# Selective-scan mixer: y and the gate computed transposed, norm weights folded into the output weights, score rings of three banks

## What is computed

```python
gate, hBC, dt = split(x_n @ in_proj_w.T)          # 8192, 10240, 128 wide
hBC = silu(causal_conv(hBC, conv_w, 4 taps) + conv_b)
hs, Bm, Cm = hBC                                  # 128 heads of 64; 8 groups of 128
dt = clip(softplus(dt + dt_bias), 0, 100); A = -exp(A_log)
# per chunk of 128 tokens, cum = cumsum(dt * A):
Y_diag = (C B^T * exp(cum_l - cum_s), l >= s) @ (hs * dt)
Y_off  = exp(cum) * (C @ state)
Y = Y_diag + Y_off + hs * D
g = Y * silu(gate)                                # per group of 1024 columns:
out = g * rsqrt(mean(g*g) + eps) * norm_w
y = out @ out_proj_w.T
# attention, 32 heads of 16: softmax(q k^T / 4, causal) @ v
```

## Time and profile before

| | |
|---|---|
| median of 3 runs | 3235.74 us (3235.0 to 3238.88) |
| the profiled execution's own time | 3237.73 us, span 3235.9 us |
| TensorE, VectorE, ScalarE, GpSimd busy | 91%, 63%, 32%, 20% |
| TensorE clock granted, mean | 0.966 |
| mixer, 64 slots | 141 to 2320 us |
| experts, first pass | 2365 to 2480 us |
| attention, heads | 2667 to 3040 us |
| experts, second pass | 3110 to 3236 us |

### The profile page before, as it was taken

The page is one execution under the profiler, slowest core; times in us unless marked ns, Lnnn a source line. Parts: engine busy times, 40 slices in busy tenths (PEclk is TensorE's granted clock), DMA queues, the critical chain, the costliest instruction groups (busy, mean ns, idle before and its releaser), DMA issues. The chain is left out here.

```text
span 3235.9 us, 41691 instructions
## 1 busy us (share of the span) xinstructions
PE 2954.3 (91%) x12832; PEld 1668.3 (52%) x12832; DVE 2040.1 (63%) x3246; ACT 1035.7 (32%) x2401; POOL 654.9 (20%) x438
## 2 busy tenths in 40 slices
PE   3799999999999999999999999999879978888889
PEld 2455555555555555555555555555468443333478
DVE  5666666666666676666666676675364647777464
ACT  1233233233233233233333232232221325666421
POOL 1222132222212222221221222222121000000021
PEclk7899999999999999999999999999989888999989
DMA  4001010010001001001010100100010420111000
GB/s 164 15 2 37 1 56 24 14 56 14 23 13 45 24 13 56 15 23 55 2 35 4 56 25 13 55 1 2 10 60 0 164 75 30 37 37 34 6 7 20
DMA packets 55890, 106.97 MB, mean 33 GB/s; under 512 B 24385, under 2 KB 27537, under 8 KB 53009
## 3 DMA queue, kind: packets, MB, share of 16 engines
q1 hardware_dynamic: 50384, 102.60, 9.4%
q10 hardware_dynamic: 5312, 2.00, 0.3%
HBM read 85.71 MB, written 18.87 MB: 32 GB/s over the span
## 5 line engine op out<-in xcount | busy, mean ns | idle before, releaser
L443 PE MATMUL bank<-xnT,wh 128*128 128x512 f32 x1280 | 571.7, 598 | 60.7 <-DVE sg L832 30.0
L587 PE MATMUL bank<-wo,ggT 128*128 128x512 f32 x1024 | 469.5, 613 | 20.2 <-ACT ggT L697 20.2
L535 PE MATMUL bank<-wg,xnT 128*128 128x512 f32 x1024 | 462.2, 594 | 0.0
L443 PEld LDWEIGHTS bank<-xnT,wh 128*128 128x128 f32 x1280 | 236.4, 191 | 332.3 <-issue 290.4
L739 DVE SCALAR_TENSOR_TENSOR cacc<-raw,cwh,cacc 128x512 f32<-128x512 f32 x480 | 390.3, 813 | 17.0
L587 PEld LDWEIGHTS bank<-wo,ggT 128*128 128x128 f32 x1024 | 199.9, 197 | 271.6 <-issue 271.6
L535 PEld LDWEIGHTS bank<-wg,xnT 128*128 128x128 f32 x1024 | 185.1, 191 | 184.5 <-issue 184.5
L510 PEld LDWEIGHTS bank<-xch,em 128*128 128x128 f32 x2048 | 237.4, 194 | 53.6 <-issue 52.0
L915 POOL TENSOR_TENSOR yt<-yt,hd 128x1024 f32<-128x1024 f32 x64 | 153.2, 2394 | 471.9 <-DVE yt L804 407.6
L510 PE MATMUL bank<-xch,em 128*128 128x64 f32 x2048 | 243.5, 278 | 5.1 <-DVE em L781 1.1
L645 ACT COPY xs<-bank 128x512 f32<-128x512 f32 x128 | 74.5, 582 | 522.4 <-PE bank L469 522.4
(11 more groups left out here) (240 smaller groups left out, 4476.2 us busy)
## 6 DMA issues: line engine op xcount, KB each, us to landing
wh<-w_hs_dram SPq DMA_DIRECT2D x80, 256.0 KB, 3.0
wg<-w_gate_dram SPq DMA_DIRECT2D x8, 2048.0 KB, 7.8
wo<-w_out_dram SPq DMA_DIRECT2D x8, 2048.0 KB, 8.0
qk_scratch<-at_part SPq DMA_DIRECT2D x48, 256.0 KB
at_qT<-qk_scratch SPq DMA_DIRECT2D x32, 192.0 KB, 2.6
at_kT<-qk_scratch SPq DMA_DIRECT2D x32, 192.0 KB, 2.6
wgu<-w_gu_dram SPq DMA_DIRECT2D x1, 3584.0 KB, 11.2
at_wa<-w_attn_dram SPq DMA_DIRECT2D x1, 3072.0 KB, 10.4
```

Of the source, the lines that this page charges most:

```text
L443: mm = nc.tensor.matmul(BA[bank][:, :], wh[:, j, k, :], xnT[:, k, h * HALF:(h + 1) * HALF], start=(k == 0), stop=(k == KC - 1))
L535: mm = nc.tensor.matmul(BA[b][:, :], xnT[:, k, ttok], wg[:, k, u * 512:(u + 1) * 512], start=(k == 0), stop=(k == KC - 1))
L587: mm = nc.tensor.matmul(BA[b][:, :], ggT[:, j, :], wo[:, j, :], start=(j == 0), stop=(j == JT - 1))
```

## The change

Y and the gate are kept transposed: 128 of the group's columns on the partitions, tokens along the row, in eight blocks j. The diagonal product has xch as weights (64 columns) and em streaming (128 columns), and even and odd heads write the lower and the upper 64 partitions. The off-diagonal product and the gate become products of 128 columns, 8 and 32 a slot. The transposes of y and the copies ggT are gone, yt is the output product's weights. norm_w is multiplied into the output weights once a group, by GpSimd in slot z=0 (po_weigh, before the taps). exp(cum) is wanted as rows: it is stored by head in DRAM, and SyncE loads it for each slot, each head's row broadcast over 64 partitions, into EC (load_decay), on the semaphore of the decay rows and after the off-diagonal multiply of the slot before. D comes as a column per partition (Ds), and hd is made from act2, not from xs. The mean of squares now sums over partitions: ScalarE squares yt, VectorE sums over j (sqs), and a product with a column of ones ends it on TensorE, after the output product. The mask product is gone: ScalarE takes Relu(-x), then exp(-x), and the mask 0/1 is multiplied into B C^T (dv_small).

In the attention both score rings have three banks, released piece by piece; GpSimd splits the maxima, and the row transposes stand one step later.

```diff
@@ pe_diff, pe_slot @@
             for q in quarters:
-                ac_ex.wait(pe, 4 * n + q - 1)
-                nc.tensor.matmul(BD[q % 2][:, :], identb[:, :], negq[:, :], start=True, stop=False)
+                ac_mn.wait(pe, 4 * n + q - 1)
...
-                        mm = nc.tensor.matmul(BY[u][:, (hh % 8) * HP:(hh % 8 + 1) * HP],
-                                              em[:, q, i * P:(i + 1) * P], xch[:, hh * HP:(hh + 1) * HP],
+                        side, j = hh % 2, hh // 2 % 4
+                        mm = nc.tensor.matmul(BY[u][side * HP:(side + 1) * HP, j * P:(j + 1) * P],
+                                              xch[:, hh * HP:(hh + 1) * HP], em[:, q, i * P:(i + 1) * P],
                                               start=True, stop=True)
...
-                for k in range(KC):
-                    mm = nc.tensor.matmul(BA[b][:, :], xnT[:, k, ttok], wg[:, k, u * 512:(u + 1) * 512],
-                                          start=(k == 0), stop=(k == KC - 1))
+                for i in range(4):
+                    j = 4 * u + i
+                    for k in range(KC):
+                        mm = nc.tensor.matmul(BA[b][:, i * P:(i + 1) * P], wg[:, k, j * P:(j + 1) * P], xnT[:, k, ttok],
+                                              start=(k == 0), stop=(k == KC - 1))
...
-            dv_gg.wait(pe, n + 1)
-            for u in range(2):
-                if not last:
-                    ac_xs.wait(pe, 2 * n + 3 + u)
-                for i in range(4):
-                    mm = nc.tensor.transpose(BT[(5 * (z + 1) + 3 + u) % 2][:, i * P:(i + 1) * P],
-                                             yt[:, (4 * u + i) * P:(4 * u + i + 1) * P], ident[:, :])
-                mm.then_inc(pe_yT.sem, 1)
             tile(2)
             tile(3)
-            pe.wait_ge(d_wo, 16 * g + 16)
+            pe.wait_ge(wo_set, 17 * g + 17)
...
             b = bank()
+            dv_gg.wait(pe, n + 1)
             for j in range(JT):
-                if j % 4 == 0:
-                    ac_yT.wait(pe, 2 * n + j // 4 + 1)
-                mm = nc.tensor.matmul(BA[b][:, :], ggT[:, j, :], wo[:, j, :], start=(j == 0), stop=(j == JT - 1))
+                mm = nc.tensor.matmul(BA[b][:, :], yt[:, j * P:(j + 1) * P], wo[:, j, :], start=(j == 0), stop=(j == JT - 1))
             mm.then_inc(pe_out.sem, 1)
+            dv_sq.wait(pe, n + 1)
+            if not last:
+                ac_xs.wait(pe, 2 * n + 3)
+            nc.tensor.matmul(BT[1][:, 0:1], sqs[:, :], ones1[:, :], start=True, stop=True).then_inc(pe_ss.sem, 1)
@@ ac_exps, dv_slot, GpSimd, SyncE @@
-                nc.scalar.activation(em[:, q, :], BD[q % 2][:, :], ACT.Exp).then_inc(ac_ex.sem, 1)
+                nc.scalar.activation(em[:, q, :], BD[q % 2][:, :], ACT.Relu, scale=-1.0).then_inc(ac_mn.sem, 1)
+            for q in quarters:
+                ac_mn.wait(act, 4 * n + q + 1)
+                nc.scalar.activation(em[:, q, :], em[:, q, :], ACT.Exp, scale=-1.0).then_inc(ac_ex.sem, 1)
...
             if not last:
                 dv_masked(dve, *nxt)
+            ac_sq.wait(dve, n + 1)
+            pe_ss.wait(dve, n)
+            nc.vector.tensor_reduce(sqs[:, :], sq.rearrange("p (j t) -> p t j", j=JT), AX, ALU.add).then_inc(dv_sq.sem, 1)
...
+        def po_weigh(pool, g):
+            pool.wait_ge(wo_set, 17 * g + 16)
+            pool.wait_ge(d_pk[0], 48 * g + 48)
+            nc.gpsimd.tensor_tensor(wo[:, :, :], wo[:, :, :], nw[:, 0, :].unsqueeze(2).broadcast_to([P, JT, C]),
+                                    ALU.mult).then_inc(wo_set, 1)
...
-            ac_xs.wait(pool, 2 * n + 2)
-            pool.wait_ge(d_pk[h], 32 * g + 32)
+            pool.wait_ge(d_pk[h], 48 * g + 48)
+            dv_act.wait(pool, (2 * g + h) * PT + PT)
             po_y3.wait(pool, n)
-            nc.gpsimd.tensor_tensor(headed(hd[:, :]), headed(xs[:, :]), per_head(h, c, O_D), ALU.mult).then_inc(po_hd.sem, 1)
+            nc.gpsimd.tensor_tensor(hd[:, :].rearrange("p (j t) -> p j t", j=JT), act2[:, h, 0:JT, c * P:(c + 1) * P],
+                                    Ds[:, h, :].unsqueeze(2).broadcast_to([P, JT, P]),
+                                    ALU.mult).then_inc(po_hd.sem, 1)
...
+                def load_decay(g, z):
+                    for side in range(2):
+                        sp.dma_start(EC[64 * side:64 * side + 64, :].rearrange("p (j t) -> p j t", j=JT),
+                                     ecum_dram[bass.ds(g * HG, HG), z * P:(z + 1) * P].rearrange("(j s) t -> s j t", s=2)
+                                     [side:side + 1].broadcast_to([64, JT, P])).then_inc(d_rw, 16)
...
                     pe_df.wait(sp, 4 * (8 * g + z + 1))
                     sp.sem_inc(turned, 1)
+                    if z > 0:
+                        dv_yo.wait(sp, skip_first(g, z, 2) + 2)
                     if z < NT - 1:
                         load_rows(g, z + 1)
+                        load_decay(g, z + 1)
@@ attention @@
-            BST = [BANK[0:2], BANK[2:4]]
-            BS = BANK[4:6]
+            BST, BS = BANK[0:3], BANK[3:6]
...
-            v_mx.wait(pe, S1_FROM[NT] * h + m - 1)
+            v_mx.wait(pe, MX * h + m - (2 if m >= 3 else 3))
...
-                            if i == 1 and (not known or h < AH - 1):
+                            if i == 2 and (not known or h < AH - 1):
                                 m_rows(h + 1)
...
+                        nc.gpsimd.tensor_tensor(part(0), nm[:, k, :], one[:, :], ALU.mult).then_inc(po_mp.sem, 1)
+                        po_mp.wait(pool, 4 * h + 1)
+                        nc.gpsimd.tensor_tensor(nr[:, k, :], nm[:, k, :], part(0), ALU.subtract).then_inc(po_mp.sem, 1)
```

More of the change, by code:

```diff
@@ L41 @@
 PR = PARTS * HG
[L43 to L44 removed]
+O_DT, O_DEC, O_LAST = 0, HG, 2 * HG
+PACK = 3 * HG
 DT_MAX = 100.0
@@ L363, in _ @@
                     chain(nc.vector.tensor_copy(pack[:, :, :, O_DT:O_DT + HG], z4(dt[:, :])))
-                    chain(nc.vector.tensor_copy(pack[:, :, :, O_D:O_D + HG],
-                                                rows[:, 2, :].rearrange("p (g h) -> p g h", g=G).unsqueeze(1)
-                                                .broadcast_to([P, NT, G, HG])))
+                    for side in range(2):
+                        half = slice(64 * side, 64 * side + 64)
+                        o = nc.vector.tensor_copy(Dc[half, :, :], rows[half, 2, :].rearrange("p (g j s) -> p s g j", g=G, s=2)[:, side])
+                    chain(o)
                     dve.wait_ge(a_ch, 5)
@@ L389, in mixer @@
         sg = sb(ctx, "sg", [P, GC])
-        ggT = sb(ctx, "ggT", [P, JT, P])
-        junk = sb(ctx, "junk", [P, GC], BF16)
+        EC = sb(ctx, "EC", [P, GC])
+        sqs = sb(ctx, "sqs", [P, P])
+        ones1 = sb(ctx, "ones1", [P, 1])
         em = sb(ctx, "em", [P, NQ, QH * P])
@@ L496, in pe_slot @@
                     dv_st.wait(pe, skip_last(g, z - 1, 2) + u + 1)
-                    nc.tensor.matmul(BY[u][:, :], act2[:, h, JC, tok], st[:, u * 512:(u + 1) * 512],
-                                     start=True, stop=True).then_inc(pe_yo.sem, 1)
+                    for i in range(4):
+                        mm = nc.tensor.matmul(BY[u][:, i * P:(i + 1) * P], st[:, (4 * u + i) * P:(4 * u + i + 1) * P],
+                                              act2[:, h, JC, tok], start=True, stop=True)
+                    mm.then_inc(pe_yo.sem, 1)
             dv_xc.wait(pe, n + 1)
@@ L689, in ac_slot @@
                 tanh(0)
-            act.wait_ge(d_pk[h], 32 * g + 32)
-            for u in range(2):
-                pe_yT.wait(act, 2 * n + u + 1)
-                if u == 0:
-                    pe_out.wait(act, n)
-                for i in range(4):
-                    j = 4 * u + i
-                    o = nc.scalar.activation(ggT[:, j, :], BT[(5 * (z + 1) + 3 + u) % 2][:, i * P:(i + 1) * P],
-                                             ACT.Copy, scale=nw[:, h, j:j + 1])
-                o.then_inc(ac_yT.sem, 1)
             copy(2)
@@ L748, in dv_silu_tile @@
                 if h == 0:
+                    po_hd.wait(dve, 8 * p[0] - 4)
                     pe_hs.wait(dve, 2 * (8 * p[0] - 4))
@@ L751, in dv_silu_tile @@
                 else:
+                    po_hd.wait(dve, 8 * p[0])
                     pe_hs.wait(dve, 2 * 8 * p[0])
@@ L776, in dv_masked @@
             n = 8 * g + z
-            dv_sm.wait(dve, n + 1)
+            dv_sm.wait(dve, 2 * n + 2)
             for q in range(NQ):
@@ L1728, in attention @@
             S1_FROM = [sum(len(pieces(0, (k + 1) * P)) for k in range(i)) for i in range(NT + 1)]
-            assert S1_FROM[NT] % 2 == 0
+            NS_ = S1_FROM[NT]
+            MX = NS_ + 1
+            S2_FROM = [sum(len(pieces(k * P, T)) for k in range(j)) for j in range(NT + 1)]
+            assert NS_ % 3 == 0 and S2_FROM[NT] == NS_
             with nc.Block() as block:
@@ L1777, in take, with split, first, body @@
                             .then_inc(po_v.sem, 1)
```

(28 more changed lines are left out.)

177 lines of the change are left out of this document (87 added, 90 removed).

## The result

The changed kernel takes 3081.06 us (median of four, 3079.58 to 3087.84) against 3237.27 for the kernel before beside it: a ratio of 0.952, with an interval of 0.951 to 0.954. I had forecast 3038, with a range of 2985 to 3135. So the direction and the range held, but the gain is 156 us where I had 198. The profiled execution is the longest of the four and has a span of 3086.0 (3235.9 before); its reading shows which terms were off.

The account below looks back on a forecast made before the run. TensorE, busy 91% of the span near full clock, was taken to bound the kernel. From 3235.9 us, -189 in the mixer, +3 for prologue and end, -12 in the attention gave 3038; range 2985 to 3135.

Parts of the forecast that it names:

- Unit prices: TensorE float32 passes: 0.43 us for 512 columns, 0.112 for 128 with own weights; diagonal product near 2.0 a slot.
- the prediction's estimate of 25 ns: Overhead on each of 3744 added TensorE passes, from the skill page's 60 cycles: 94 us less of a gain.
- Ordinary slots: 30 mixer slots with three projection tiles: -2.2 us each, -66 in all, with 1.9 waiting before the first tile.
- The reduction: VectorE's sum over j: 1.2 us, ending 0.7 us before the output product in ordinary slots.
- z=7: Seven mixer slots without tiles: 16.6 us down to 13.4, -3.1 each, -22 in all.
- z=3 and z=4: z=3 and group 7's z=4 to 6 (11 slots): -5.7 us each, -63; other z=4 (7): -2.8, -20.
- the rival of the shared semaphore: Decay products wait for EC's load: cost begins at landing 9 us after issue, 3486 us at 17; chance 0.03.
- z=0: Eight slots with the 7.6 us weighting on GpSimd holding VectorE's gate product; reduction 0.9 us late: -1.9 each, -15.
- Attention: Heads from 11.40 to 11.0 us, -12 over 31 heads; bounds nothing and -80.
- Clock: Slots z=3: half of a 1.6 us clock loss comes back; wrong if mixer mean clock is under 0.97.
- The sum: 3235.9 (span) - 189 (mixer) + 3 (prologue and end) - 12 (attention) = 3038 us.
- a low clock before the first tile: Rival: clock falls in the longer wait before the first tile, 3.1 us in 30 slots, 3131 us; chance 0.08.

## Why the prediction was right, and where it was not

- **Unit prices: right.** A pass every 0.112 us in the gate product, and a diagonal product of 1.97 for 2.0. The Trainium skill's 60 cycles a matmul (TensorEngine Tiling (Array Packing), Instruction Overhead) stand against 5 ns more than a quarter of a 512-column pass; read as a cost on top of each pass, as in the prediction's estimate of 25 ns, this trace doesn't agree with that page. What the figure means for products of few columns no run tests.
- **Ordinary slots: right in mechanism, 0.65 us a slot too careful.** I had the first tile at +16.3 us, of which 1.9 waiting. The +14.45 at which TensorE would want it doesn't follow from the terms given, which make 14.6, with 1.7 of waiting; the -2.2 a slot doesn't use it. It came at +15.7 (1253.03 less the off-diagonal product's start at 1237.3), with 1.02 of waiting: hd cost the convolution 1.5 us, not 1.9, which is 0.4 of the 0.6; TensorE alone would have come there at +14.7. The mechanism was shown by moving hd: the wait goes. Slots z=5 that waited for EC brought the mean from 33.6 to 34.0.
- **The reduction: mis-sized, 1.90 for 1.2.** It costs nothing in ordinary slots, but in slots z=7 it ends only 0.2 us before the output product does, and with that the next step failed.
- **z=7: wrong, +9.4 for -22 us.** I took the slot's stream and removed its parts, and read no cost for the loop, since the earlier trace rows show none on TensorE. The step that failed is that the new sum-of-squares product is a wait at the very end of the loop. I had called it hidden because I only asked when the reduction ends, not what stands behind the wait. The waits of VectorE in the trace of the kernel before hold the warning, a row that I didn't bring forward:

```profile
DVE yt L806 <- issue: 26.9, 6, 5.0
```

VectorE was already standing there six times, for 4.3 to 5.0 us, without a releaser, at the same back edge.
- **z=3 and z=4: right but for the rival.** Without EC's wait they have 24.0 and 35.9, for forecasts of 24.4 (30.1 less 5.7) and 35.9 (38.7 less 2.8). The 13 and 11 us missing are the rival of the shared semaphore, to which I gave 0.03. The mistake was to take a landing time from a queue that carries nothing else, and an answer for all slots from one kind of slot.
- **z=0: wrong, -3.5 for -15.** The missing term is the clock after the back edge: 1.7 us on the diagonal product in six slots, 10 of the 11.5 us. The six went from 38.6 to 39.0; most of the -3.5 is group 0's slot (44.1 to 39.0), and group 7's, at full clock, went from 38.6 to 37.6. The weighting took 7.0 us for 7.6 and cost 0.85 us a slot, where I had 0.9, but that is luck: its hold fell on xch ahead of the first tile, and was over before the gate product on which I had put it.
- **Attention: -19 for -12.** The heads went to 10.78 for 11.0. The run with the attention alone shows that this is the attention's own gain; how it divides between the rings of three banks and GpSimd's small steps isn't shown.
- **Clock.** It was forecast to come back in slots z=3; in those without a wait for EC it did (24.0). The mean over the mixer is 0.98 (0.99 before), above the 0.97 that I had named as a sign of being wrong.
- **The sum: within the range, partly by luck.** In the profiled span the mixer gave 60 us less than forecast, the attention (20.5 from its first head to its last) 8 more, and the rest 4 more. The range reached 97 us up for a low clock before the first tile in every ordinary slot, which didn't happen (that stretch of tiles takes 7.13 us, as before); EC's 41 us and the back edge's 31 had no place in it and happened to fit.

## What to carry to other kernels

Count loads on one semaphore only if the same instruction needs them all: a shared one cost 41 us here. A new wait at the end of a loop body is dear if little is queued behind it, however short it is, because the branch back then stands in the open and the clock falls behind it; ask of every added wait what lies between it and the back edge. Take a load's landing time from a stretch in which its queue carries the same neighbours.

## What the runs showed of the hardware

The branch back of the loop leaves TensorE idle for 4.8 to 5.6 us at each of six crossings (30.8 us in all) when its last wait has only the one-column product behind it; with 3.7 us of products behind the last wait 0.2 to 1.9 remain, with 6.2 us nothing, and without a loop nothing. In two halves of the output partitions 64-column float32 passes come every 0.06 us, in one half every 0.11, and it doesn't take strict alternation: runs of eight passes to one half cost 0.2 us in 32. A GpSimd operation over SBUF holds VectorE's two-input operations for as long as it lasts: xch took 1.23 us by itself, 5.34 and 8.07 under the weighting, depending on when it starts. It also goes the other way: hd, started 1.7 us into VectorE's gate product, took 2.88 us for 1.90. The first agrees with the Trainium skill's page SBUF — State Buffer, section Who interferes with whom, by which a VectorE instruction with two inputs in SBUF contends with a GpSimd instruction that reads there, and the contention is an exclusive lock. After waits of 2.3 to 5.5 us TensorE's next product ran partly or nearly wholly at the lower level of its clock: 8.78 us for 7.1 (granted clock 0.81), 3.68 for 1.97 (0.51); after waits of 1.4 to 1.9 at the back edge the diagonal product had its 1.97.
